# GpSimd forms the difference of the real and the imaginary spectrum once a step, and layer 0's first matmul reads it

## The chip, the cores and the metric

The kernel runs on one core of a Trainium2 chip. The metric is the device time of one execution in microseconds; the number quoted for a kernel is the median of its runs. Besides, one execution is profiled, and all durations below come from that one.

## The reference, cut to what matters

Two spectral layers run one after the other on an image tensor of 4 x 45 x 90 x 384 (batch, height, width, channel). The channels fall into 8 blocks of 48.

```python
# layer 0
f  = fft2(x, axes=(1, 2), norm='ortho')
Xh = f.real - f.imag                      # only 23 of the kw columns are kept
o1 = relu(einsum('bhwni,nio->bhwno', Xk, w1[0]) + b1[0])
o2 = einsum('bhwni,nio->bhwno', o1, w2[0]) + b2[0]
x  = ifft2(softshrink(o2), ...).real + x
# layer 1
xf  = rfft2(x); xr, xi = xf.real, xf.imag
o1r = relu(xr@w1[0] - xi@w1[1] + b1[0]);  o1i = relu(xi@w1[0] + xr@w1[1] + b1[1])
o2r = softshrink(o1r@w2[0] - o1i@w2[1] + b2[0]);  o2i = softshrink(o1i@w2[0] + o1r@w2[1] + b2[1])
out = irfft2(o2r + 1j*o2i) + x
```

Layer 0's first product needs only the difference of the real and the imaginary part. The kernel stays in the spectrum between the layers: layer 1's spectrum is layer 0's input spectrum with the real part of layer 0's result added.

## The kernel before, in words

The work is cut into 8 tasks (4 batches by 2 halves of 192 channels), and each task into 6 steps of 4 columns kw of the spectrum, the last one of 3 (`STEP`, `kws(s)`). There are so 48 steps, 8 of them short. All data are float32. One list, `order`, made by `schedule()` (L103), is walked by every engine, and each engine issues its own part of each entry, so an engine's queue is in the order of the list. The entries are:

- `fwd`: the DFT along the width on TensorE (PE, L566), copied by ScalarE (ACT, L401) into `fs` and stored to a scratch in DRAM by SyncE (SP).
- `load` and `a`: SP loads the rows of a step into `bt`, PE makes the DFT along the height (L612), and ACT (L410) and VectorE (DVE, L482) copy one half each of the channel pairs into `xs[s % 2]`. Its last axis holds 45 real values and then 45 imaginary ones.
- `c0`: layer 0's first product (L630). Four 64 x 64 matmuls, one for each block of a half task, take the real half with the weights `w10[0]`, and four more take the imaginary half with `w10[1]`, which is the negated copy that DVE makes once (L469, tile `w10_neg`, "w_neg" in the rows). They accumulate in two PSUM banks. ACT (L416) and DVE (L486) make the relu into `o10`.
- `d0`: layer 0's second product (L641), four matmuls on `o10`, of the same shape as one half of `c0`. ACT (L421) and DVE (L494 to L504) shrink it into `nt`. Then GpSimd (POOL, L362) subtracts `nt`, which holds the negated result, from the real half of `xs`.
- `c1`, `d1`: layer 1's two products (L653, L666), with relu by ACT (L428) and DVE (L511), and shrinking by ACT (L435) and DVE (L519) into `ns`.
- `t`: transposes of `nt` (L679), added to `ns` by DVE (L527).
- `e`: inverse DFT along the height (L692), copied by ACT (L441) and DVE (L534), stored to a scratch.
- `rows`, `inv`: the inverse DFT along the width (L599), added to the image by DVE (L545). POOL issues the store of each chunk of 8 image rows (L371) and, once an earlier chunk's store has landed, the load of a later task's rows into the same place (`refill`, L352). The first six steps each also issue a load of a third image from POOL (L365).

A profile counts two records for each float32 matmul, so a line of four matmuls shows as x8.

Within step s the list is: load(s+2), c1(s-1), inv, e(s-2), inv, c0(s), d1(s-1), d0(s), fwd, fwd, a(s+1), fwd, fwd, t(s-1), inv; the `fwd` entries are there in three steps of six and the `inv` entries in others. So PE has t, c1, e and perhaps inverse work between `a` of a step and `c0` of the same step:

```python
        if s < NSTEPS:
            order.append(("c0", s))
        if 0 < s <= NSTEPS:
            order.append(("d1", s - 1))
        if s < NSTEPS:
            order.append(("d0", s))
```

The first step is different: the list begins with all of task 0's `fwd`, load(0), load(1), a(0), then c0(0), d0(0), a(1), c1(0), c0(1), d1(0), with nothing between a(0) and c0(0).

## Time and profile before

| | |
|---|---|
| median of 3 runs | 551.11 us (551.05 to 554.34) |
| the profiled execution's own time | 549.69 us |
| its span in the profile | 547.9 us |
| PE busy | 506.0 us, 92% |
| DVE / ACT / POOL busy | 56% / 38% / 25% |
| mean granted clock | 0.97 of full |

The profiled execution's time is 1.8 us above its span, and 1.4 us below the median. A row's line number (L630) is a line of the kernel before. PE is the matmuls, PEld its weight loads, "idle before" the time an engine sat idle just before an instruction, with what released it. Busy time of matmuls that overlap is counted once, while the mean of one is its full length in the pipeline.

### The profile page before, as it was taken

To read this page: it belongs to the slowest core of one execution; us is meant where nothing else is said; L and a number is where in the kernel's file an instruction comes from. 1 tells how busy PE (TensorE), PEld (TensorE's weight loads), DVE (VectorE), ACT (ScalarE), POOL (GpSimd) and SP (SyncE) were. 2 spreads that over 40 slices of the span, in tenths; PEclk is the share of its full clock that TensorE was granted. 3 is DMA by queue.
4 is the path that set the end of the run, shared out by engine and by line. 5 is a ranking of instruction groups with operands and counts; after the bars stand their busy time and mean duration, and the time that the engine had idled before them with its cause. 6 is when DMAs were issued, how large, how long until landed. Compare 5 with 4: busy or idle time off the path is not lost.

```text
span 547.9 us, 14234 instructions
## 1 busy us (share of the span) xinstructions
PE 506.0 (92%) x5824; PEld 372.7 (68%) x5824; DVE 305.5 (56%) x675; ACT 210.9 (38%) x473; POOL 135.6 (25%) x146
## 2 busy tenths in 40 slices
PE   4559999999999999999999999999999999999763
PEld 1147777767777777777777777777777777887521
DVE  6414455456754667456763577456764577556643
ACT  0015544553344433554245433444345434343201
POOL 9701211012330132212331133211331111111124
PEclk9759999999999999999999999999999999999978
DMA  8869764576889578886889588886889655633388
GB/s 184 260 155 245 204 173 109 112 206 173 237 214 239 147 192 246 212 203 173 251 200 228 156 205 237 220 200 168 249 202 220 178 159 150 152 95 101 107 222 252
DMA packets 76717, 104.60 MB, mean 191 GB/s; under 512 B 7761, under 2 KB 63303, under 8 KB 76526
## 3 DMA queue, kind: packets, MB, share of 16 engines
q1 hardware_dynamic: 57622, 55.97, 38.9%
q0 software_dynamic: 10608, 40.45, 28.4%
q10 hardware_dynamic: 8424, 7.28, 5.2%
q8 instruction: 47, 0.77, 0.6%
q14 instruction: 16, 0.13, 0.1%
HBM read 52.23 MB, written 51.43 MB: 189 GB/s over the span
## 4 chain that ended last, share of the span: by engine, by line
PE 84%; DVE 5%; DMA 3%; POOL 3%; ACT 2%; issue 2%; SPq 0%; POOLq 0%; ACTq 0%; DVEq 0%
PE ps L666 15%; PE ps L599 13%; PE ps L566 11%; PE ps L692 11%; PE ps L653 11%; PE ps L612 9%; PE ps L630 7%; PE ps L679 5%; PE ps L641 3%; DVE img L545 2%; DMA scr_f<-fs 2%; DVE ns L519 1%; POOL img L379 1%; ACT p L435 1%; POOL xs L362 1%
## 5 line engine op out<-in xcount | busy, mean ns | idle before, releaser
L545 DVE TENSOR_TENSOR img<-ps,img 90x768 f32<-90x768 f32 x92 | 82.7, 900 | 21.7 <-PE ps L599 17.0
L362 POOL TENSOR_TENSOR xs<-xs,nt 128x360 f32<-128x360 f32 (+1 forms) x48 | 41.5, 864 | 212.1 <-DVE nt L497 134.2
L599 PE MATMUL ps<-jr,cst 64*128 64x384 f32 (+1 forms) x358 | 82.5, 528 | 6.7 <-DVE img L545 5.9
L666 PE MATMUL ps<-wt,o 128*109 128x96 f32 (+1 forms) x768 | 85.4, 263 | 0.1
L666 PEld LDWEIGHTS ps<-wt,o 128*109 128x109 f32 (+1 forms) x768 | 76.4, 171 | 13.3 <-issue 12.5
L519 DVE SCALAR_TENSOR_TENSOR ns<-p,ps 109x384 f32<-109x384 f32 x96 | 53.1, 553 | 57.2 <-ACT p L435 57.2
L566 PE MATMUL ps<-img,cst 128*64 128x384 f32 (+1 forms) x368 | 74.0, 520 | 11.4 <-DMA img<-x 7.6
L612 PEld LDWEIGHTS ps<-cst,bt 128*64 128x64 f32 x1472 | 63.2, 141 | 20.6 <-issue 13.9
L371 POOL DMA_DIRECT2D y<-img x42 | 34.7, 827 | 170.7 <-DVE img L545 170.7
L428 ACT ACTIVATE o<-ps,wt 97x180 f32<-97x180 f32 (+1 forms) x96 | 33.8, 406 | 108.8 <-PE ps L653 108.8
L612 PE MATMUL ps<-cst,bt 128*64 128x90 f32 x1472 | 69.0, 248 | 6.3 <-DMA bt<-scr_f 6.3
L692 PE MATMUL ps<-ns,cst 64*90 64x192 f32 x736 | 70.9, 322 | 0.0
L653 PE MATMUL ps<-xs,wt 64*97 64x180 f32 (+1 forms) x768 | 67.7, 313 | 2.8 <-POOL xs L362 2.5
L692 PEld LDWEIGHTS ps<-ns,cst 64*90 64x90 f32 x736 | 62.6, 155 | 7.7 <-issue 1.5
L653 PEld LDWEIGHTS ps<-xs,wt 64*97 64x97 f32 x768 | 56.7, 159 | 13.3 <-POOL xs L362 6.7
L435 ACT ACTIVATE p<-ps 109x384 f32<-109x384 f32 x96 | 47.1, 491 | 38.4 <-PE ps L666 38.4
L566 PEld LDWEIGHTS ps<-img,cst 128*64 128x64 f32 x368 | 25.5, 144 | 40.7 <-issue 34.8
L511 DVE TENSOR_SCALAR o<-ps,wt 97x180 f32<-97x180 f32 (+1 forms) x96 | 33.7, 393 | 32.6 <-PE ps L653 32.6
L401 ACT ACTIVATE fs<-ps 112x384 f32<-112x384 f32 x84 | 39.1, 476 | 33.3 <-PE ps L566 26.9
L482 DVE COPY xs<-ps 128x360 f32<-128x360 f32 (+1 forms) x48 | 24.8, 516 | 44.0 <-PE ps L612 44.0
L527 DVE TENSOR_TENSOR ns<-ps,ns 109x192 f32<-109x192 f32 x96 | 29.8, 352 | 33.5 <-PE ps L679 32.7
L599 PEld LDWEIGHTS ps<-jr,cst 64*128 64x128 f32 x358 | 31.8, 190 | 24.1 <-issue 12.0
(43 smaller groups left out, 411.9 us busy)
## 6 DMA issues: line engine op xcount, KB each, us to landing
y<-img POOLq DMA_DIRECT2D x35, 540.0 KB, 5.1
img<-x POOLq DMA_DIRECT2D x30, 540.0 KB, 8.3
scr_i<-et SPq DMA_DIRECT2D x48, 270.0 KB, 5.8
scr_f<-fs SPq DMA_DIRECT2D x176, 72.0 KB, 3.0
bt<-scr_f SPq DMA_DIRECT2D x40, 270.0 KB, 4.6
jr<-scr_i SPq DMA_DIRECT2D x48, 216.0 KB, 5.3
img<-x ACTq DMA_DIRECT2D x10, 540.0 KB, 6.7
y<-img SPq DMA_DIRECT2D x11, 270.0 KB, 3.6
```

What stands on the lines that cost most here:

```text
L362: nc.gpsimd.tensor_tensor(re, re, nt[s % 2][:, :, 0:kws(s), 0:H], ALU.subtract).then_inc(re_ok, 1)
L401: nc.scalar.activation(fs[k][0:rows, 0:cols], ps[0:rows, P3 + g % 2, 0:cols], ACT.Copy).then_inc(f_cp, 1)
L435: nc.scalar.activation(p1[0:rows, p, :], ps[0:rows, P2 + p, 0:2 * HC], ACT.Relu).then_inc(d1_p, 1)
L519: nc.vector.scalar_tensor_tensor(out=ns[0:rows, p].rearrange("p n r c -> p (n r c)"), in0=p1[0:rows, p, :], scalar=2 * LAM, in1=ps[0:rows, ...
L545: nc.vector.tensor_tensor(y, p, y, ALU.add).then_inc(i_add, 1)
L566: last = mm(ps[64 * r:64 * r + 64, P3 + g % 2, 0:(b - a) * HC], K["w_fwd"], img[t % IMGS][:, a:b, :].rearrange("p h c -> p (h c)"), start= ...
L599: last = mm(ps[:, B0 + r, 0:n], K["w_inv"][64 * r:64 * r + 64, :], set_rows(t, j)[64 * r:64 * r + 64, at, 0:n], start=True, stop=True)
L612: last = mm(ps[64 * ab:64 * ab + 64, P0 + q, k * 2 * H:(k + 1) * 2 * H], bt[s % BT][:, at:at + 64], K["h_fwd"], start=True, stop=True)
L630: last = mm(ps[64 * q:64 * q + 64, P1 + ab, 0:n], w10[im][k, f, q, :], xt[k, q, 0:kws(s), im * H:(im + 1) * H], start=im == 0, stop=im == 1)
L653: last = mm(ps[0:2 * BS + 1, P2 + ab, q * STEP * H:q * STEP * H + n], w1[k, im, 2 * f + q, :], xt[k, q, 0:kws(s), im * H:(im + 1) * H], st ...
L666: last = mm(ps[0:rows, P2 + p, b * 2 * BS:(b + 1) * 2 * BS], o11[:, b, 2 * p:2 * p + kw, :].rearrange("p k m -> p (k m)")[:, 0:rows], w21[ ...
L692: last = mm(ps[0:2 * H, P0 + r, p * HC:(p + 1) * HC], K[("h_inv_re", "h_inv_im")[im]][k, :], ns[k, p, :, im, :], start=im == 0, stop=im == 1)
```

## The change

Once a step, in the `a` entry, POOL waits for both copies into `xs` and subtracts the imaginary half from the real half into a new tile `xd` (128 x 360 values, 128 x 270 in a short step). `c0` waits for that difference alone and runs four matmuls on it instead of eight on the two halves; the negated weights and the instruction that made them are gone. POOL's older subtraction from `xs` (in `d0`) loses its own two waits on the copies, which now stand ahead of it in POOL's queue. The difference is one buffer: the next one is written after `a` of the next step, which on PE comes behind the `c0` that reads it.

```diff
--- before.py
+++ after.py
@@ -168,7 +168,7 @@
         for n, m in WCOLS.items():
             V[n] = wt[:, at:at + m]
             at += m
-        w10 = [V["w10"].rearrange("p (f q o) -> p f q o", f=HALVES, q=2), sb("w10_neg", [128, HALVES, 2, 64])]
+        w10 = V["w10"].rearrange("p (f q o) -> p f q o", f=HALVES, q=2)
         w20 = V["w20"].rearrange("p (f q o) -> p f q o", f=HALVES, q=2)
         w1 = V["w1"].rearrange("p (r n o) -> p r n o", r=2, n=HALVES * 2)
         w21 = V["w21"].rearrange("p (n o) -> p n o", n=NBLK)
@@ -176,6 +176,7 @@
         fs = [sb(f"fs{k}", [128, 2 * HC]) for k in range(FS)]
         bt = [sb(f"bt{k}", [128, STEP * HC + 16]) for k in range(BT)]
         xs = [sb(f"xs{k}", [128, 2, STEP, 2 * H]) for k in range(2)]
+        xd = sb("xd", [128, 2, STEP * H])
         o10 = sb("o10", [128, 2, STEP * H])
         p0 = sb("p0", [128, 2, STEP * H])
         ev = sb("ev", [128, 2, H])
@@ -204,6 +205,7 @@
         f_st = [sem(f"f{k}_stored") for k in range(FS)]
         b_ld = [sem(f"b{k}_loaded") for k in range(BT)]
         a_mm, a_act, a_dve = sem("a_product"), sem("a_copied_act"), sem("a_copied_dve")
+        xd_ok = sem("re_minus_im")
         c0_mm, c0_act, c0_dve = sem("c0_product"), sem("c0_relu_act"), sem("c0_relu_dve")
         d0_mm, d0_p, d0_ss, d0_ev, d0_sym, re_ok = (sem("d0_product"), sem("d0_clipped"), sem("d0_shrunk"), sem("d0_kw0_shrunk"),
                                                   sem("d0_kw0_even"), sem("re_added"))
@@ -352,10 +354,15 @@
                     pool.dma_start(img[k][0:W, r0:r1, :], x[b, r0:r1, :, f * HC:(f + 1) * HC].rearrange("h w c -> w h c")).then_inc(x_ld[k][c], 16)
 
             for kind, *what in order:
-                if kind == "d0":
+                if kind == "a":
                     s, = what
                     pool.wait_ge(a_act, s + 1)
                     pool.wait_ge(a_dve, s + 1)
+                    xt = xs[s % 2][:, :, 0:kws(s), :]
+                    nc.gpsimd.tensor_tensor(xd[:, :, 0:kws(s) * H].rearrange("p q (k m) -> p q k m", m=H), xt[:, :, :, 0:H], xt[:, :, :, H:2 * H],
+                                            ALU.subtract).then_inc(xd_ok, 1)
+                if kind == "d0":
+                    s, = what
                     pool.wait_ge(d0_ss, 2 * s + 2)
                     pool.wait_ge(d0_sym, 2 * (s // STEPS + 1))
                     re = xs[s % 2][:, :, 0:kws(s), 0:H]
@@ -466,7 +473,6 @@
                 if kind == "load" and what[0] == 0:
                     dve.wait_ge(c_ld, 16)
                     dve.wait_ge(w_ld, 16)
-                    nc.vector.tensor_scalar(w10[1][:], w10[0], -1.0, None, ALU.mult).then_inc(w_ok, 1)
                     v = w20[:, :, :, 0:BS].rearrange("p f n o -> p (f n) o")
                     nc.vector.tensor_scalar(v, v, K["lam"], 0.5, ALU.add, ALU.mult).then_inc(w_ok, 1)
                     v = w1[0:112, 1, :, 0:BS]
@@ -475,7 +481,7 @@
                     nc.vector.tensor_scalar(v, v, K["sign"][0:2 * BS, :], None, ALU.mult).then_inc(w_ok, 1)
                     v = w21[2 * BS:2 * BS + 1, :, :]
                     nc.vector.tensor_scalar(v, v, LAM, None, ALU.add).then_inc(w_ok, 1)
-                    dve.wait_ge(w_ok, 5)
+                    dve.wait_ge(w_ok, 4)
                 if kind == "a":
                     s, = what
                     dve.wait_ge(a_mm, 2 * s + 2)
@@ -614,21 +620,18 @@
                         last.then_inc(a_mm, 1)
                 if kind == "c0":
                     s, = what
-                    n, f, xt = kws(s) * H, s // STEPS % HALVES, xs[s % 2]
+                    n, f = kws(s) * H, s // STEPS % HALVES
                     if s == 0:
-                        pe.wait_ge(w_ok, 5)
-                    pe.wait_ge(a_act, s + 1)
-                    pe.wait_ge(a_dve, s + 1)
+                        pe.wait_ge(w_ok, 4)
+                    pe.wait_ge(xd_ok, s + 1)
                     if s > 0:
                         pe.wait_ge(d0_ss, 2 * s)
                     if s > 1:
                         pe.wait_ge(t_add, 2 * s - 2)
-                    for im in range(2):
-                        for ab in range(2):
-                            for q in range(2):
-                                k = slice(64 * ab, 64 * ab + 64)
-                                last = mm(ps[64 * q:64 * q + 64, P1 + ab, 0:n], w10[im][k, f, q, :], xt[k, q, 0:kws(s), im * H:(im + 1) * H],
-                                          start=im == 0, stop=im == 1)
+                    for ab in range(2):
+                        for q in range(2):
+                            k = slice(64 * ab, 64 * ab + 64)
+                            last = mm(ps[64 * q:64 * q + 64, P1 + ab, 0:n], w10[k, f, q, :], xd[k, q, 0:n], start=True, stop=True)
                     last.then_inc(c0_mm, 1)
                 if kind == "d0":
                     s, = what
```

PE's queue in one middle step, in issue order: t (L679), c1 (L653), inverse groups (L599), e (L692), c0 (L630), d1 (L666), d0 (L641). Before:

```order
L679 MATMUL ps<-cst,nt 109x128 x4
L653 MATMUL ps<-xs,wt 97x180 x8
L599 MATMUL ps<-jr,cst 128x384 x2
L692 MATMUL ps<-ns,cst 90x192 x8
L599 MATMUL ps<-jr,cst 128x384 x2
L630 MATMUL ps<-xs,wt 64x180 x4
L630 MATMUL ps<-xs,w_neg 64x180 x4
L666 MATMUL ps<-wt,o 109x96 x8
L641 MATMUL ps<-o,wt 64x180 x4
```

The same place on PE now; c0 is L634, d1 L669, d0 L644:

```order
L682 MATMUL ps<-cst,nt 109x128 x4
L656 MATMUL ps<-xs,wt 97x180 x8
L605 MATMUL ps<-jr,cst 128x384 x2
L695 MATMUL ps<-ns,cst 90x192 x8
L605 MATMUL ps<-jr,cst 128x384 x2
L634 MATMUL ps<-xd,wt 64x180 x4
L669 MATMUL ps<-wt,o 109x96 x8
L644 MATMUL ps<-o,wt 64x180 x4
```

The four matmuls with the negated weights are gone, and nothing else moved on PE.

POOL's queue over the start of the inverse work of a task, before: the subtraction of `nt` (L362), stores of image chunks (L371) and refills (L352):

```order
L362 TENSOR_TENSOR xs<-xs,nt 128x8x45
L371 DMA y<-img 90x8x192
L352 DMA img<-x 90x8x192
L362 TENSOR_TENSOR xs<-xs,nt 128x8x45
L371 DMA y<-img 90x8x192
L352 DMA img<-x 90x8x192
L371 DMA y<-img 90x8x192
L352 DMA img<-x 90x8x192
L362 TENSOR_TENSOR xs<-xs,nt 128x2x3x45
L371 DMA y<-img 90x8x192
```

The same place on POOL now; L362 is the new difference into `xd`, L369 the subtraction of `nt`, L378 the store, L354 the refill:

```order
L369 TENSOR_TENSOR xs<-xs,nt 128x8x45
L362 TENSOR_TENSOR xd<-xs 128x360
L378 DMA y<-img 90x8x192
L354 DMA img<-x 90x8x192
L369 TENSOR_TENSOR xs<-xs,nt 128x8x45
L362 TENSOR_TENSOR xd<-xs 128x2x135
L378 DMA y<-img 90x8x192
L354 DMA img<-x 90x8x192
L378 DMA y<-img 90x8x192
L354 DMA img<-x 90x8x192
L369 TENSOR_TENSOR xs<-xs,nt 128x2x3x45
L362 TENSOR_TENSOR xd<-xs 128x360
```

One difference for the next step stands directly behind each subtraction of `nt`, ahead of the stores and refills that follow.

POOL's first instructions of the main loop, now (L372 is the load of the third image, L365 before):

```order
L362 TENSOR_TENSOR xd<-xs 128x360
L369 TENSOR_TENSOR xs<-xs,nt 128x8x45
L372 DMA img<-x 90x8x192
L362 TENSOR_TENSOR xd<-xs 128x360
L369 TENSOR_TENSOR xs<-xs,nt 128x8x45
L372 DMA img<-x 90x8x192
```

The first difference has nothing ahead of it but the clears, and the second stands behind the issue of a load.

## Rows read from the trace of the kernel before

**Rows 1.** The page: busy time of each engine, and the chain by engine and line
```profile
PE 506.0 (92%) x5824; PEld 372.7 (68%) x5824; DVE 305.5 (56%) x675; ACT 210.9 (38%) x473; POOL 135.6 (25%) x146
...
PE 84%; DVE 5%; DMA 3%; POOL 3%; ACT 2%; issue 2%; SPq 0%; POOLq 0%; ACTq 0%; DVEq 0%
PE ps L666 15%; PE ps L599 13%; PE ps L566 11%; PE ps L692 11%; PE ps L653 11%; PE ps L612 9%; PE ps L630 7%; PE ps L679 5%; PE ps L641 3%; DVE img L545 2%; DMA scr_f<-fs 2%; DVE ns L519 1%; POOL img L379 1%; ACT p L435 1%; POOL xs L362 1%
```

**Rows 2.** Windows, 100 us each: busy us of PE, PEld, DVE, ACT, POOL, clock, DMA share, GB/s
```profile
200.00:300.00 100.00, 99.17 (x1190) 74.26 (x1190) 58.58 (x134) 43.31 (x98) 25.84 (x31) 1.00 0.84 213
...
400.00:500.00 100.00, 98.16 (x1220) 76.01 (x1217) 59.24 (x140) 42.89 (x97) 17.52 (x22) 1.00 0.63 161
```

**Rows 3.** Chain that ended last, 279 to 294 us: start us, us on the chain, what
```profile
283.24 0.78 PE ps L630 x16
284.01 1.90 PE ps L666 x16
285.92 0.47 PE ps L641 x8
```

**Rows 4.** Same chain, 252 to 270 us, a step of three columns kw
```profile
265.16 0.62 PE ps L630 x16
...
267.48 0.39 PE ps L641 x8
```

**Rows 5.** Groups by line and shape: busy us, mean ns, idle before and its releaser
```profile
L362 POOL TENSOR_TENSOR xs<-xs,nt 128x360 f32<-128x360 f32 x40 | 35.7, 892 | 197.8 <-DVE nt L497 132.3 <-DVE nt L504 45.5 <-ACT xs L410 19.9
...
L630 PE MATMUL ps<-xs,w_neg 64*64 64x180 f32 x320 | 19.9, 317 | 0.0
```

**Rows 6.** Timeline, 83 to 90 us: start us, us, engine, line, operation, idle before
```profile
84.35 0.49 DVE L497 SCALAR_TENSOR_TENSOR nt<-p,ps 128x135 f32<-128x135 f32 x2
...
85.09 0.73 POOL L362 TENSOR_TENSOR xs<-xs,nt 128x270 f32<-128x270 f32 x1 [6.16 <-ACT xs L410]
85.15 0.53 DVE L482 COPY xs<-ps 128x360 f32<-128x360 f32 x1 [0.30 <-PE ps L612]
...
85.77 0.82 POOL L365 DMA_DIRECT2D img<-x  x1
...
85.87 1.17 PE L653 MATMUL ps<-xs,wt 64*97 64x135 f32 x16
...
87.09 0.62 DVE L511 TENSOR_SCALAR o<-ps,wt 97x135 f32<-97x135 f32 x2 [0.71 <-PE ps L653]
...
88.28 0.54 PE L630 MATMUL ps<-xs,wt 64*64 64x180 f32 x8
```

**Rows 7.** Chain in the first steps, columns as in rows 3
```profile
35.11 1.51 PE ps L630 x16
...
37.19 0.88 PE ps L641 x8
```

**Rows 8.** Timeline of the first steps, columns as in rows 6
```profile
34.43 0.53 DVE L482 COPY xs<-ps 128x360 f32<-128x360 f32 x1 [7.16 <-PE ps L612]
...
39.76 0.89 POOL L362 TENSOR_TENSOR xs<-xs,nt 128x360 f32<-128x360 f32 x1 [16.08 <-DVE nt L504]
40.59 0.96 POOL L365 DMA_DIRECT2D img<-x  x1
...
42.23 0.54 PE L630 MATMUL ps<-xs,wt 64*64 64x180 f32 x8
42.36 0.72 ACT L428 ACTIVATE o<-ps,wt 97x180 f32<-97x180 f32 x2 [2.37 <-PE ps L653]
```

**Rows 9.** Windows of 2 us in the first steps, columns as in rows 2
```profile
38.00:40.00 2.00, 2.00 (x30) 2.00 (x28) 0.96 (x6) 0.94 (x2) 0.24 (x1) 0.50 0.29 56
...
42.00:44.00 2.00, 1.86 (x28) 1.32 (x25) 1.12 (x3) 1.13 (x3) 0.00 (x0) 1.00 0.91 232
```

**Rows 10.** Waits: engine, line, for whom: us in total, times, longest us
```profile
POOL img L352 <- DMA y<-img: 18.3, 7, 4.1
...
PEld ps L653 <- POOL xs L362: 6.7, 16, 0.8
```

## Prediction, made before the changed kernel ran

> **What bounds the kernel now.** I read the page's busy times and its chain of waits first [rows 1]: PE is busy 92% of the span and holds 84% of the chain that ended last; no other engine has more than 5% of it. L630, the line that the change cuts, has 7% of the chain. An average over stages can mislead, so the windows come next [rows 2]: between 200 and 300 us PE is busy for 99.2 us and between 400 and 500 us for 98.2, both at the full granted clock (1.00, the 2.4 GHz level). The middle of the program is all like that, so PE's own order of work is the bound, and what counts is how much sooner PE's next instruction starts. Busy time can't give that, since these matmuls overlap: one of L630 takes some 0.31 us from end to end [rows 5], while sixteen of them hold the chain for 0.78 us [rows 3]. The chain in order of time is the view that gives the pitch, and I take the sum from it.
>
> **Part 1, removed: half of c0's matmuls.** In a full step c0 holds the chain for 0.78 us (283.24, x16 records), then d1's L666 follows [rows 3]. What will eight records of this shape take? d0 is just that: four matmuls, 64 x 64 weights, 180 columns, no accumulation. It holds the chain for 0.47 us (285.92, x8) [rows 3]. Half of 0.78 would be 0.39, but a row of the right count and shape stands in the same trace, so I take 0.47: a saving of 0.31 us a step. The next line after d0 is another than after c0; I take the same handover. In a short step the two are 0.62 and 0.39 us [rows 4], a saving of 0.23. Of the 48 steps the first two are priced by themselves below; 38 full and 8 short ones are left: 38 x 0.31 + 8 x 0.23 = 11.8 + 1.8 = 13.6 us. A reader who took the busy time of the removed group would say 19.9 us for the 40 full steps alone [rows 5], some 23 us with the short ones; that counts the pipeline's fill and drain, which lie beside the neighbours' work, and I keep it only as the far end of what is possible. The near end is 0: that these matmuls already ran in the shadow of the others.
>
> **Part 2, added: POOL's difference.** It has the same 128 x 360 values and two inputs as the subtraction at L362, 892 ns each [rows 5], so I take 0.89 us, some 42 us of POOL time in all, against POOL's 25% busy now. It costs time only if c0 has to wait for it. The step with the least room behind the first two is the one at 85 us [rows 6]. POOL ends its subtraction of `nt` at 85.09 + 0.73 = 85.82, and its next item is the issue of a load (85.77, 0.82), which ends at 86.59; DVE's copy into `xs` has ended at 85.68. The difference then runs to 86.59 + 0.89 = 87.48, and c0 starts at 88.28: 0.8 us are left. Only the first six steps issue such a load. I went through all steps behind them the same way, and the room is 1.8 us at the least and 5.0 at the most. The cover is PE's own t, c1 and e, which stand between `a` and c0; if it were gone, each step would pay up to 0.89 us plus the start of an instruction, 0.25 us (DVE's last part of `nt` ends at 84.35 + 0.49 = 84.84, POOL starts at 85.09 [rows 6]), and the gain would turn into a loss.
>
> **What is queued behind the new wait on POOL.** Behind it stand the store of a finished image chunk, the refill, and the next subtraction of `nt`, for which c1 waits (PEld, 6.7 us in 16 waits [rows 10]). The new wait is for copies that are made before that step's t and c0, and every store behind it needs an inverse product that PE makes later than `a`. So the wait is over before a store is due, and a store goes out at most one difference (0.89 us) late; the images have most of a task's time to land. The refills wait for landed stores (18.3 us in 7 waits, the longest 4.1 [rows 10]), but in the queue they stand ahead of the subtraction of `nt` already today, and the difference comes right behind that one: what would delay it delays c1 first, and PE hardly waits there. I cost it at 0, with half a microsecond as the other end.
>
> **Part 3, the first two steps.** Nothing stands between a(0) and c0(0), so there the difference is bare. DVE's copy ends at 34.43 + 0.53 = 34.96 [rows 8] and c0 starts at 35.11 [rows 7]. Now: 34.96, plus 0.25 until POOL starts, plus 0.89, plus 0.05 until PE starts (85.82 to 85.87 [rows 6]) is 36.15, so +1.04. At the half clock of this stretch (0.50 from 38 to 40 us, the 1.2 GHz level [rows 9]) the cut is worth more: c0 holds the chain for 1.51 us and the eight records of d0 for 0.88 [rows 7], so -0.63. Step 0 nets +0.41. In step 1, POOL's subtraction (39.76, 0.89) and the issue of a load behind it (40.59, 0.96) [rows 8] both move by 0.41, so that the load is issued at 41.96; the difference ends at 42.85, and c0 starts at 42.90 where without the wait it would start at 42.64: +0.26. Its own cut of 0.31 is of no use in full, since d1 must wait for layer 1's relu anyway (42.36 + 0.72 = 43.08 [rows 8], now 0.41 later). I take +0.4 us for both steps together. The clock could make it dearer: it stands at 0.50 until 40 us and at 1.00 from 42 on, behind a stretch in which PE was nearly always busy [rows 9]. The microsecond of idle PE at 35 us may move the rise. Were 4 us more spent at the half clock, that would cost 2 us. That is my upper end for it, and I take 0.
>
> **Part 4, small things.** The one DVE instruction for the negated weights lies in a stretch where PE waits for the first load; it is worth 0. PE's wait for one semaphore in place of two is worth 0 as well, because no idle time of PE at L630 shows in the chain. DVE's and ACT's relus of c0 need to be ready for d0, which stands behind d1's 1.90 us [rows 3]; c0 shorter by 0.31 does not touch that. d1 itself needs layer 1's relus: DVE ends them at 87.09 + 0.62 = 87.71 [rows 6], and d1 starts behind c0 at 88.28 + 0.78 = 89.06. Being 0.31 us sooner leaves a microsecond. So nothing is late next.
>
> **The sum.** -13.6 + 0.4 = -13.2 us. Against the profiled execution's own 549.69 us that is 536.5. The median of the runs shown, 551.11, is 1.4 us above that execution; taken from it the result is 537.9 us, my forecast, 2.4% less. No change can be told from a difference under about 1%, 5.5 us.
>
> **Rivals.** (a) *DVE is blocked while POOL reads SBUF.* This is the one on the other side. If each difference held up a DVE instruction on which PE waits, for its whole 0.89 us, 48 of them would cost 42.7 us, and the time would be 537.9 + 42.7 = 580.6. It decides from 13.2 / 48 = 0.28 us a step on. The place would be t's additions (L527) or an inverse addition (L545), which come just behind `a`. For it: POOL's share grows from 25% to some 33%, and the steps put the difference there. Against it: DVE's copy at 85.15 ran its whole length beside POOL's subtraction (85.09 to 85.82) and took 0.53 us [rows 6]; at 34.43, with POOL idle, it took 0.53 us too [rows 8]. The Trainium skill ("SBUF — State Buffer", "SBUF: two separate sides") says that a GpSimd op and a DVE op with two SBUF inputs, or in a two-port mode, exclude each other for their whole length. By that rule the DVE operations here that read PSUM are free, with which the row agrees; only the two small additions of `ev` in every sixth step have two SBUF inputs, and they stand ahead of POOL's work.
>
> (b) *Other waits appear once PE is quicker*, so that half of the gain is given back: 551.1 - 6.6 = 544.5. For it: PE waits now and then for POOL's subtraction [rows 10]; the chain holds 5% of DVE and 3% of POOL [rows 1], and DMA is busy up to 84% in the middle [rows 2]. Against: those waits hang on d0, d1 and inverse products, which all move together with c0, and PE is idle for no more than 1.8% of the middle stretches [rows 2].
>
> (c) *The removed matmuls cost nothing*, since a new matmul is let in by something else than the count: 551.1 + 0.4 = 551.5. For it: four blocks lie in different quarters of the array and overlap. Against: d0's 0.47 against c0's 0.78 on the same chain [rows 3].
>
> (d) *The gain is larger*, toward the busy time: 551.1 - 23 + 0.4 = 528.5. Against: the same two rows.
>
> **Chances.** Forecast 0.82; (b) 0.09; (c) 0.04; (a) 0.03; (d) 0.02. The range runs from 534.5 (a saving of 0.36 a step, no price at the start, and the scatter of a median) to 543.0 (the late clock, the delayed stores, and most of (b)). Faster by over 1% (under 545.6): 0.92, the forecast, (d) and most of (b). Within 1%: 0.05. Slower: 0.03.
>
> **What would show it.** Right: L634 holds the chain for 0.47 us with x8 records where L630 held it for 0.78; c0 never waits for POOL but in the first two steps; POOL's new line is 0.89 us each; DVE's L482, L527 and L545 keep their lengths; PE stays above 98% busy in the middle at clock 1.00. Wrong: PE idle before L634 with POOL as the releaser in most steps (then the room was misread), longer DVE operations (rival a), PE idle at t or c1 that was not there before (b), or a chain in which L634 still holds 0.7 us (c).

## The result

| | before | changed |
|---|---|---|
| median | 552.54 us (551.05 to 554.34, 4 runs) | 536.11 us (535.78 to 537.09, 4 runs) |
| the profiled execution's own time | 549.69 us | 537.09 us |
| its span | 547.9 us | 535.3 us |

The ratio is 0.9704 with a 95% interval of 0.9664 to 0.9745: the change makes the kernel 3.0% faster. The forecast was 537.9 us with a range of 534.5 to 543.0, so the time lies in the range, 1.8 us under the forecast. The two profiled executions differ by 12.6 us and the medians by 16.4: the profiled run of before is 2.9 us under its median, that of the changed kernel 1.0 over its own. The experiments say part of why. Ratios and spreads here are of fast runs alone; three slow runs of the kernel before (558.05, 559.73 and 1225.76 us, all in later sessions) are left out.

The page of the changed kernel, busy times and the chain by engine and line:

```profile
PE 492.0 (92%) x5440; PEld 359.2 (67%) x5440; DVE 304.1 (57%) x674; ACT 209.5 (39%) x473; POOL 172.9 (32%) x194
...
PE 83%; DVE 5%; DMA 5%; POOL 2%; issue 2%; ACT 2%; SPq 0%; POOLq 0%; DVEq 0%; ACTq 0%
PE ps L669 15%; PE ps L605 13%; PE ps L572 12%; PE ps L695 12%; PE ps L656 11%; PE ps L618 9%; PE ps L682 5%; PE ps L634 4%; PE ps L644 3%; DMA scr_f<-fs 2%; DVE img L551 2%; DVE ns L525 2%; POOL xs L369 1%; ACT p L442 1%; DVE nt L503 1%
```

PE is 92% busy as before [rows 1], over a span shorter by 12.6 us; POOL went from 25% to 32%. The changed line, L634 now, has 4% of the chain where L630 had 7%.

The windows of 100 us, columns as in [rows 2]:

```profile
200.00:300.00 100.00, 99.22 (x1140) 73.75 (x1141) 59.69 (x138) 44.40 (x101) 32.06 (x39) 1.00 0.84 219
...
400.00:500.00 100.00, 97.14 (x1144) 73.98 (x1143) 61.83 (x140) 42.37 (x98) 24.59 (x30) 1.00 0.58 153
```

PE is the bound as before, at the full granted clock. The prediction wanted it above 98% in both windows; in the second it is 97.14, because the 1.28 us for which PE waits behind the last d0 (at 494.3 us now, 507.7 before) have moved into that window. The chain in the middle, to be held against [rows 3]:

```profile
277.33 0.47 PE ps L634 x8
277.79 1.70 PE ps L669 x16
279.49 0.47 PE ps L644 x8
```

L634 holds the chain for 0.47 us with x8 records (0.78 with x16 before), and d0 behind it (L644) for 0.47 as it did. The short step, against [rows 4]:

```profile
259.81 0.39 PE ps L634 x8
```

The timeline of the step with the least room, against [rows 6]:

```profile
84.13 0.49 DVE L503 SCALAR_TENSOR_TENSOR nt<-p,ps 128x135 f32<-128x135 f32 x2
...
84.70 0.73 POOL L369 TENSOR_TENSOR xs<-xs,nt 128x270 f32<-128x270 f32 x1 [5.08 <-DVE nt L503]
...
84.93 0.53 DVE L488 COPY xs<-ps 128x360 f32<-128x360 f32 x1 [0.30 <-PE ps L618]
85.37 0.82 POOL L372 DMA_DIRECT2D img<-x  x1
...
85.49 1.17 PE L656 MATMUL ps<-xs,wt 64*97 64x135 f32 x16
...
86.21 0.83 POOL L362 TENSOR_TENSOR xd<-xs 128x360 f32<-128x360 f32 x1
...
87.89 0.54 PE L634 MATMUL ps<-xd,wt 64*64 64x180 f32 x8
```

The difference (L362 now) is done at 87.04 and L634 starts at 87.89: 0.85 us of room, where 0.8 was forecast. One thing was not forecast: POOL's subtraction (L369) starts at 84.70, 0.08 us behind its last input (84.13 + 0.49 = 84.62). Before, it was 0.25 us [rows 6].

I took the start of d0's first weight load in each of the 48 steps of both profiles and compared step by step (steps counted from 0). Most full steps are 0.31 to 0.34 us shorter and the short ones 0.23. Steps 44 to 46, and 6, are 0.45 to 0.48 shorter, and the short steps 5 and 47 by 0.39 and 0.38. Steps 18 and 25 are 0.44 and 0.53 shorter. Step 15 gains 0.16, and steps 12 and 31 only 0.05; in these two PE has a wait at c1 (L656) that it did not have before. One of them, step 12:

```profile
143.02 0.81 POOL L354 DMA_DIRECT2D img<-x  x1 [2.12 <-DMA y<-img]
...
143.84 0.74 POOL L369 TENSOR_TENSOR xs<-xs,nt 128x270 f32<-128x270 f32 x1
...
144.64 1.17 PE L656 MATMUL ps<-xs,wt 64*97 64x135 f32 x16 [0.51 <-POOL xs L369]
```

POOL's refill waited 2.12 us for a store to land, and so its subtraction, for which c1 waits, came late. In the second profile of the changed kernel this step is 0.32 shorter, like the others. The other one is step 31: PE waits 0.28 us at 334.85, since the subtraction starts 0.44 us behind its last input where it starts 0.15 behind it in the like steps; it starts as DVE's copy ends. That is so in experiments 1, 2, 10 and 11 too, and why is open.

By stretches, in us, with the second profile of the changed kernel (the first experiment):

| stretch | before | changed | changed, again |
|---|---|---|---|
| to a(0) | 31.64 | 31.28 | 31.35 |
| a(0) to d0(1) | 13.25 | 14.71 | 13.49 |
| d0(1) to d0(2) | 10.26 | 9.94 | 9.94 |
| d0(2) to d0(46), 44 steps | 442.72 | 428.91 | 428.59 |
| d0(46) to d0(47) | 9.33 | 8.95 | 8.94 |
| d0(47) to the end | 40.70 | 41.51 | 41.16 |
| span | 547.9 | 535.3 | 533.5 |

### The profile page after: what moved, and what is told of

Its sections match the earlier page's. It is cut to its first block, busy times and chain, and to the rows that moved or that the text cites. A ratio compares the mean times of both kernels' runs of the same rounds, so it can differ in the third digit from the quotient of the medians.

```text
span 535.3 us, 13467 instructions
## 1 busy us (share of the span) xinstructions
PE 492.0 (92%) x5440; PEld 359.2 (67%) x5440; DVE 304.1 (57%) x674; ACT 209.5 (39%) x473; POOL 172.9 (32%) x194
## 4 chain that ended last, share of the span: by engine, by line
PE 83%; DVE 5%; DMA 5%; POOL 2%; issue 2%; ACT 2%; SPq 0%; POOLq 0%; DVEq 0%; ACTq 0%
PE ps L669 15%; PE ps L605 13%; PE ps L572 12%; PE ps L695 12%; PE ps L656 11%; PE ps L618 9%; PE ps L682 5%; PE ps L634 4%; PE ps L644 3%; DMA scr_f<-fs 2%; DVE img L551 2%; DVE ns L525 2%; POOL xs L369 1%; ACT p L442 1%; DVE nt L503 1%
## 5 line engine op out<-in xcount | busy, mean ns | idle before, releaser
L369 POOL TENSOR_TENSOR xs<-xs,nt 128x360 f32<-128x360 f32 (+1 forms) x48 | 41.6, 866 | 160.0 <-DVE nt L503 130.6
L605 PE MATMUL ps<-jr,cst 64*128 64x384 f32 (+1 forms) x358 | 84.2, 540 | 6.9 <-DVE img L551 5.6
L669 PE MATMUL ps<-wt,o 128*109 128x96 f32 (+1 forms) x768 | 85.2, 263 | 0.5 <-DVE o L517 0.5
L669 PEld LDWEIGHTS ps<-wt,o 128*109 128x109 f32 (+1 forms) x768 | 76.3, 171 | 13.3 <-issue 12.6
L572 PE MATMUL ps<-img,cst 128*64 128x384 f32 (+1 forms) x368 | 72.2, 507 | 13.3 <-DMA img<-x 7.7
L378 POOL DMA_DIRECT2D y<-img x42 | 34.6, 825 | 132.4 <-DVE img L551 132.1
L656 PE MATMUL ps<-xs,wt 64*97 64x180 f32 (+1 forms) x768 | 68.9, 317 | 2.4 <-POOL xs L369 2.3
L656 PEld LDWEIGHTS ps<-xs,wt 64*97 64x97 f32 x768 | 57.5, 161 | 13.3 <-POOL xs L369 6.7
L362 POOL TENSOR_TENSOR xd<-xs 128x360 f32<-128x360 f32 (+1 forms) x48 | 38.0, 792 | 34.4 <-DVE xs L488 34.3
```

Source lines behind the costliest of these rows:

```text
L362: nc.gpsimd.tensor_tensor(xd[:, :, 0:kws(s) * H].rearrange("p q (k m) -> p q k m", m=H), xt[:, :, :, 0:H], xt[:, :, :, H:2 * H], ALU.subtr ...
L369: nc.gpsimd.tensor_tensor(re, re, nt[s % 2][:, :, 0:kws(s), 0:H], ALU.subtract).then_inc(re_ok, 1)
L572: last = mm(ps[64 * r:64 * r + 64, P3 + g % 2, 0:(b - a) * HC], K["w_fwd"], img[t % IMGS][:, a:b, :].rearrange("p h c -> p (h c)"), start= ...
L605: last = mm(ps[:, B0 + r, 0:n], K["w_inv"][64 * r:64 * r + 64, :], set_rows(t, j)[64 * r:64 * r + 64, at, 0:n], start=True, stop=True)
L656: last = mm(ps[0:2 * BS + 1, P2 + ab, q * STEP * H:q * STEP * H + n], w1[k, im, 2 * f + q, :], xt[k, q, 0:kws(s), im * H:(im + 1) * H], st ...
L669: last = mm(ps[0:rows, P2 + p, b * 2 * BS:(b + 1) * 2 * BS], o11[:, b, 2 * p:2 * p + kw, :].rearrange("p k m -> p (k m)")[:, 0:rows], w21[ ...
```

## The experiments

**1. The changed kernel again.** No edit.

> The changed kernel itself, timed in one session with the next three and with the kernel before. By the traces the step saves 0.31 us 38 times and 0.23 us 8 times and the first two steps lose 1.5 us, so 12 to 13.5 us less than before (ratio 0.975 to 0.978). If the medians' 16.4 us are real and not scatter of the kernel before, the ratio is 0.970 again.

Measured: 536.28 us, ratio 0.9709 (0.9672 to 0.9746). The second alternative came true: the ratio is 0.970 again. But the stretch with the 44 steps is 428.59 us, 14.1 less than in the profile of before, while the ratio makes 16 us. The rest lies outside these profiles, in runs of before that are slower than its profiled one (see experiment 5).

**2. The difference formed, and read by nobody.** The kernel before, with

```diff
+                if kind == "a":
+                    s, = what
+                    pool.wait_ge(a_act, s + 1)
+                    pool.wait_ge(a_dve, s + 1)
+                    if s > 0:
+                        pool.wait_ge(xd_ok, s)
+                    nc.gpsimd.tensor_tensor(xd ..., re, im, ALU.subtract).then_inc(xd_ok, 1)
                 if kind == "d0":
                     s, = what
-                    pool.wait_ge(a_act, s + 1)
-                    pool.wait_ge(a_dve, s + 1)
```

> The kernel before, with GpSimd forming the difference of each step at the same place in its queue, but nobody reads it: the first product still runs eight matmuls on the two halves. Theory (the difference is hidden and slows no other engine): within 1 us of the kernel before, DVE's copy at 0.53 us, its additions at 0.62 us a pair and 0.95 us as before. Rival (DVE is blocked while GpSimd reads SBUF): DVE operations beside the difference grow by up to 0.83 us, and the time by over 5 us.

Measured: 550.4 us, ratio 0.9961 (0.993 to 0.9992). The groups by line and shape of this kernel:

```profile
L555 DVE TENSOR_TENSOR img<-ps,img 90x768 f32<-90x768 f32 x84 | 79.8, 953 | 21.0 <-PE ps L609 16.3
...
L364 POOL TENSOR_TENSOR xd<-xs 128x360 f32<-128x360 f32 x40 | 32.8, 820 | 35.8 <-ACT xs L420 22.6 <-DVE xs L492 10.7 <-issue 2.4
...
L537 DVE TENSOR_TENSOR ns<-ps,ns 109x192 f32<-109x192 f32 x88 | 27.7, 353 | 33.4 <-PE ps L689 32.7
...
L492 DVE COPY xs<-ps 128x360 f32<-128x360 f32 x40 | 21.3, 532 | 44.4 <-PE ps L622 44.4
```

The difference takes 0.82 us, and DVE's copy (532 ns), its additions behind the transposes (353) and behind the inverse (953) are what they were. The rival is out for operations that read PSUM. The stretch of 44 steps is 442.43 us against 442.72, so the difference is close to free: two steps are longer, 31 by 0.26 us as in the changed kernel, and 38 by 0.58. Steps 5, 6 and 44 to 47 are 0.14 to 0.16 us shorter: the same surplus that the changed kernel shows there. The ratio says some 2 us less than before (0.4%, between 0.1 and 0.7), more than the 1 us that the theory allowed; the surplus of six steps is 0.9 us of it.

**3. Half the product alone.** The kernel before, with `for im in range(1)` in c0 and `start=True, stop=True`. It leaves out the imaginary half of layer 0's input.

> The kernel before with only the real half of the first product: four matmuls in place of eight, no difference, no new wait; it leaves out the imaginary part of layer 0's input. It prices the cut alone. Theory: 0.47 us on the chain in a full step, 0.39 in a short one, 0.6 us saved in the first step, so 14 us under the kernel before and 1 to 2 us under the changed kernel, all of that in the first two steps. Rival (GpSimd's difference costs something in the middle too): the steps from the third on are shorter than the changed kernel's by more than 0.03 us each.

Measured: 537.23 us, ratio 0.9732 (0.9693 to 0.977). Without any difference on POOL, the last steps (40 to 47) are 0.31 and 0.22 or 0.23 us shorter than before, each of them, with no surplus. So the cut is worth what the row of d0 said. The rival is out: of the steps from the third on only 12, 15 and 31 are shorter than the changed kernel's by more than 0.03 us (0.26, 0.15 and 0.26), and against its second profile only 15 and 31. Steps 18 and 25 are 0.44 and 0.51 us shorter here too, so their extra belongs to the profile of before and not to POOL. The kernel is 1.0 us slower than the changed one, not 1 to 2 us faster as the theory had it; the runs of the two overlap. Three things that the rows show go into that. The surplus of 0.15 us is missing. The stretch behind the last d0 is 43.03 us here against 41.51 and 41.16: the granted clock is 0.88 from 494 to 498 us and 0.69 from 498 to 502, where both profiles of the changed kernel have 1.00. And the start is no better. In its chain the first steps read

```profile
35.72 0.91 PE ps L630 x8
...
37.20 0.88 PE ps L641 x8
...
40.70 2.65 PE ps L653 x16
```

L653's sixteen records in step 1 last 2.65 us here, though no bare wait for POOL stands ahead of them.

**4. The first two steps as of old.** The changed kernel, with c0 of steps 0 and 1 on the two halves, waiting for the copies, and the difference from step 2 on:

```diff
-                    pe.wait_ge(xd_ok, s + 1)
+                    if s < 2:
+                        pe.wait_ge(a_act, s + 1)
+                        pe.wait_ge(a_dve, s + 1)
+                    else:
+                        pe.wait_ge(xd_ok, s - 1)
```

> The changed kernel, but the first two steps use the two halves and the negated weights as before, and the difference begins with the third step. Theory (the loss at the start comes from the bare wait for GpSimd and from the clock that rises later behind it): L653's sixteen records in step 1 last 1.6 us as before and not 2.7, and the kernel is 1.0 to 1.5 us under the changed one. Rival (the clock's rise in that stretch varies from run to run whatever the code): no difference that holds, or L653's line still at 2.7 us.

Measured: 535.18 us, ratio 0.969 (0.9649 to 0.9731), 1.1 us under the changed kernel timed beside it; the two intervals overlap for the most part, so I call it a hint. L671, layer 1's product in step 1, lasts 2.47 us: the clock rises late here too, without the bare wait. In the second profile of the changed kernel, with the bare wait, it rises early (a(0) to d0(1) in 13.49 us, table above). In the second profile of the kernel before, which has no bare wait either, it rises late (14.16 us for that stretch, 13.25 in the first; experiment 5). The rival holds: the clock's rise moves by some 2 us between profiles of one and the same kernel.

**5. The kernel before again.** No edit.

> The kernel before, profiled a second time, for where its runs scatter (549 to 557 us in the last session). Theory: the middle (from the third d0 to the 47th) is 442.7 us again within 0.3, and the scatter lies in the first 45 us and behind the last d0. Rival: the middle differs by over 1 us between two profiles, and then a saving read from one profile is not safe.

Measured: 551.76 us, ratio 0.9993. The stretch of 44 steps is 444.06 us, 1.34 more than in the first profile. The rival holds (and the start differs too, as just said), and the profile shows the place. In its chain:

```profile
221.75 0.78 PE ps L630 x14
222.53 1.18 issue
223.71 0.47 PE ps L630 x2
224.17 1.70 PE ps L666 x16
```

PE stops for 1.18 us inside c0 of step 19 (counted from 0; the expectations of experiments 9 and 10 call it 18), behind the 14th of its 16 records, and the profile shows nothing that it waits for ("issue"). Step 19 as a whole is 1.63 us longer than in the first profile. The other 43 steps are the same within 0.2 us.

**6. The waits moved alone.** The kernel before, where POOL's two waits for the copies stand in the `a` entry, with nothing else there.

> The kernel before with one thing of the change alone: GpSimd's two waits for the copies stand in the a entry, ahead of the stores, and not in front of its subtraction; no difference is formed. In the profiles so far GpSimd starts that subtraction 0.24 us (median) behind its last input where four waits stand in front of it, and 0.09 us behind it where two do. Theory (the shorter start helps where layer 1's product waits for GpSimd, some 15 to 20 steps): lag 0.09, and 1 to 2.5 us under the kernel before, like the kernel with the unread difference. Rival (that kernel's 0.4% is scatter, or the difference itself does it): no change, under 0.5 us.

Measured: 550.99 us, ratio 0.9991 (0.9967 to 1.0014). POOL's subtraction starts 0.09 us (median) behind its last input, where it was 0.24. But only steps 44 and 47 are shorter, by 0.16 and 0.14 us, where experiment 2 had six such steps. The lags say why. Where nothing stands in POOL's queue between the `a` entry and the subtraction, all four waits stand in a row again, and the lag is 0.23 or 0.24 as of old: so ahead of steps 5, 6, 45 and 46, and not ahead of 44 and 47. This settles that the surplus comes from the waits and not from the difference. The theory got the mechanism right and its worth wrong: only in these few steps does POOL's start set d0's time, and elsewhere 0.15 us there buys nothing. This profile has the gap of experiment 5 at the same instruction, and larger, and it costs more than its length:

```profile
220.59 0.77 PE ps L632 x14
221.36 2.02 issue
223.37 0.47 PE ps L632 x2
223.84 2.66 PE ps L668 x16
226.50 0.81 PE ps L643 x8
```

```profile
222.00:224.00 2.00, 0.63 (x4) 0.36 (x4) 0.12 (x1) 0.12 (x1) 0.00 (x0) 1.00 0.64 132
224.00:226.00 2.00, 2.00 (x15) 2.00 (x15) 0.69 (x2) 0.78 (x2) 0.81 (x1) 0.59 0.86 264
226.00:228.00 2.00, 2.00 (x15) 0.99 (x16) 0.82 (x3) 0.96 (x2) 0.00 (x0) 0.55 0.74 211
228.00:230.00 2.00, 2.00 (x40) 1.45 (x38) 0.48 (x2) 1.31 (x3) 0.89 (x1) 1.00 0.06 17
```

Behind 2.02 us of idle PE the mean granted clock of the next two windows is 0.59 and 0.55, so it stood at the half level (0.50, 1.2 GHz) for some 3.4 of these four microseconds, and d1 takes 2.66 us in place of 1.70. Step 19's d0 comes 3.4 us late in all.

**7. Four differences in a row.** The changed kernel; from step 8 on three more differences go into a tile of their own first:

```diff
+                    for r in range(3 if s >= 8 else 0):
+                        nc.gpsimd.tensor_tensor(xe ..., ALU.subtract).then_inc(xe_ok, 1)
+                        pool.wait_ge(xe_ok, 3 * (s - 8) + r + 1)
```

> The changed kernel, but from the ninth step on GpSimd forms the difference four times in a row, the last one being the one that is read: 2.7 to 2.8 us later. This measures the room that the prediction read from the trace. Theory: the room is about 2 us in each second step of a task (1.8 read from the kernel before, 0.2 more by the shorter start and operation), and also in the last few steps, and 3 us or more in the others; so PE waits 0.7 to 0.8 us for GpSimd in some 8 steps, 6 us in all. Rival (the room is smaller than read): waits in over 20 steps and over 15 us.

Measured: 546.13 us, ratio 0.9901 (0.9873 to 0.9929); 9.9 us over the changed kernel. From its waits:

```profile
PE ps L639 <- POOL xd L367: 10.3, 15, 1.8
```

PE waits 15 times for the difference, the 1.8 us at the start among them. Step by step against the changed kernel, seven of the theory's eight places (13, 19, 25, 37 and 43 to 45) come 0.75 to 0.79 us late, as worked out from a room of 2.0, and the eighth (31) 0.47. But six more (12, 14, 20, 26, 32, 38) are 0.5 to 1.0 us late, where I had read 3 us of room or more. The theory's 6 us became 9.9, still far from the rival's 15. POOL's timeline at the largest one:

```profile
218.59 0.82 POOL L383 DMA_DIRECT2D y<-img  x1
...
224.40 0.80 POOL L355 DMA_DIRECT2D img<-x  x1 [4.15 <-DMA y<-img]
225.22 0.90 POOL L374 TENSOR_TENSOR xs<-xs,nt 128x360 f32<-128x360 f32 x1
226.07 2.63 POOL L364 TENSOR_TENSOR xe<-xs 128x360 f32<-128x360 f32 x3
228.77 0.82 POOL L367 TENSOR_TENSOR xd<-xs 128x360 f32<-128x360 f32 x1
```

In the changed kernel the store of that stretch is issued at 215.05; here it is issued at 218.59, of which the three extra differences ahead of it make 2.6 us. The refill behind it needs a landed store and so comes at 224.40 (220.38 there), the subtraction of `nt` right behind it, and only then four more differences. The room read from a profile holds for a delay that leaves the rest of the queue where it is; one that moves the queue's stores eats more than itself.

**8. The difference on DVE.** The changed kernel, with the same `tensor_tensor` behind DVE's copy in place of POOL's. POOL's subtraction of `nt` then waits for the difference besides, so it has three waits in front of it.

> The changed kernel with the difference on VectorE, right behind its copy, in place of GpSimd. Theory: an operation of some 0.45 us, which no trace here shows yet; in steps without forward work the additions behind the transposes follow DVE's copy within 0.1 us and have 0.35 us of room before e, so they come late by 0.1 to 0.2 us in some 20 steps; the start is better by 0.4 us; 0 to 3 us slower than the changed kernel. Rival (a faster engine is the better place): up to 1 us faster.

Measured: 537.59 us, ratio 0.9745 (0.9717 to 0.9773), 1.3 us slower than the changed kernel by the medians (of two sessions). The timeline of two steps:

```profile
152.94 0.88 POOL L363 TENSOR_TENSOR xs<-xs,nt 128x360 f32<-128x360 f32 x1 [3.48 <-DVE nt L509]
...
153.31 0.90 DVE L486 TENSOR_TENSOR xd<-xs 128x360 f32<-128x360 f32 x1
...
154.14 0.61 DVE L532 TENSOR_TENSOR ns<-ps,ns 109x192 f32<-109x192 f32 x2
```

```profile
162.66 0.53 DVE L486 TENSOR_TENSOR xd<-xs 128x360 f32<-128x360 f32 x1
```

Alone the difference takes 0.53 us, shorter than POOL's 0.82. But at 153.31 it takes 0.90: POOL's subtraction runs until 153.82, and DVE's ends 0.39 us behind that. Of its 48 instances the sixteen that begin well inside such a subtraction last 0.81 to 1.06 us; four that begin in its last 0.18 us last 0.53 to 0.58, like the others. All twenty end 0.29 to 0.42 us behind the end of POOL's subtraction. So a DVE operation with two inputs in SBUF is kept out while a GpSimd one runs. The Trainium skill ("SBUF — State Buffer", "SBUF: two separate sides") says that whichever of the two starts first keeps the other out; the trace agrees for GpSimd first, and no run here has the other order. This is rival (a) of the prediction, alive in the place where its rule has it. The additions behind the transposes then start late, and in these steps d0 comes 0.05 to 0.2 us later, twice by more (0.36 and 0.67). POOL's subtraction starts 0.15 us (median) behind its last input, and steps 44 to 46 are 0.41 or 0.42 us shorter than before, so they keep 0.10 of the surplus of 0.15. The Trainium skill's "GPSIMD Engine Reference" ("Engine selection") puts elementwise work on VectorE, as GpSimd is about twice as slow with two inputs. Here it is 1.5 times as slow (0.82 against 0.53 us), and DVE's speed is of no use, for the time is set elsewhere.

**9. The old stream shifted.** The kernel before, with 32 matmuls of two columns in PE's wait for the first load:

```diff
+                    if s == 0:
+                        for r in range(32):
+                            mm(ps[0:2, P2 + r % 2, 0:2], cst[0:64, 0:2], cst[0:64, 0:2], start=True, stop=True)
```

> The kernel before with 32 tiny matmuls (128 instructions, two columns each) put into TensorE's wait for the first load, so that all later TensorE instructions stand 128 places further in its stream. Two of four profiles with the old TensorE stream show TensorE idle for 1.2 and 2.0 us at the same instruction, behind the 14th record of c0 in step 18, with nothing waited for. Theory (the next block of instructions comes late there, where the DMA engines are at their busiest): with the stream shifted no such gap at that place, runs from 549 to 552 and a median 1 to 2 us under the kernel before. Rival (the gap belongs to that moment or to the work, not to the place in the stream): the gap is at the same instruction again, or the spread of 549 to 558 us stays.

Measured: 551.79 us, ratio 0.9991 (0.9968 to 1.0013), runs from 550.1 to 554.4. The profile has no gap at that place, and its 44 steps take 443.05 us. The runs of before beside it go from 549.3 to 554.8 with a median of 552.3, 0.5 us above this kernel's, well inside the interval and less than the 1 to 2 us of the theory. a(0) starts at 33.33 here and not at 31.64, which may hide up to 1.7 us of gain. The fillers' own length is not what delays it: they were done at 27.1, and a(0) waited for the first load of `bt`, which landed later. So it is in all four kernels with fillers (32.45 to 33.57, against 30.91 to 32.25 in the ten profiles without), and why is open. Step 12 is 0.65 us longer here than in the first profile, since PE waits 0.89 us for POOL behind a refill that waited for a landed store, as in the changed kernel. The theory is neither borne out nor refuted.

**10. The new stream set back.** The changed kernel with 76 such matmuls at the same place.

> The changed kernel with 76 tiny matmuls (304 instructions) in TensorE's wait for the first load, about as many as the change removes before step 18, so that the stream around step 18 has its old alignment again. Theory (late instruction block): the gap of 1 to 2 us can come back in c0 or d1 of step 18, runs spread over 3 us or more and the median is 1 us or more above the changed kernel's 536.2 (up to 1 us of it may be the filler itself, read from the start of a(0)). Rival: no gap, spread 2 us as before.

Measured: 536.79 us, ratio 0.972 (0.9695 to 0.9746), four runs within 1.3 us; no gap. The theory's guess that the alignment alone brings the gap back fell, as far as one profile and four runs can tell. It may be that a gap needs dense transfers at that moment as well, and here c0 of step 19 comes 4.5 us earlier (216.5 against 221.0); no run shows this.

**11. Fillers for the clock.** The changed kernel with 36 matmuls of 180 columns in PE's wait for the first load and 8 ahead of the first difference.

> The changed kernel with matmuls that nobody reads in two idle stretches of TensorE at the start: 36 of 180 columns in its wait for the first load (25 to 31 us), and 8 in the bare wait for the first difference. Theory (the clock is at half speed from 31 to 41 or 43 us because TensorE was idle before): the granted clock is 1.00 from a(0) on, a(0) takes 1.3 us and not 2.7, L656's line in step 1 takes 1.6, and the time is 3 to 4 us less. Rival (the clock rises late whatever is done there, as it varied between profiles of one kernel): clock 0.50 at 32 to 40 us again and no gain; if the fillers themselves run at half speed they end near 33 us and cost up to 2 us.

Measured: 536.29 us, ratio 0.9707 (0.9681 to 0.9734): no gain. The windows of 2 us:

```profile
26.00:28.00 2.00, 2.00 (x60) 2.00 (x56) 1.27 (x4) 0.00 (x0) 0.00 (x0) 1.00 0.55 151
28.00:30.00 2.00, 0.44 (x12) 0.11 (x4) 0.00 (x0) 0.00 (x0) 0.00 (x0) 1.00 0.03 4
30.00:32.00 2.00, 0.00 (x0) 0.00 (x0) 0.00 (x0) 0.00 (x0) 0.00 (x0) 0.69 0.62 177
...
34.00:36.00 2.00, 2.00 (x29) 1.69 (x29) 0.47 (x1) 0.47 (x1) 0.00 (x0) 0.50 0.20 25
36.00:38.00 2.00, 1.57 (x20) 0.55 (x12) 0.13 (x2) 0.00 (x1) 0.82 (x1) 0.60 0.98 268
38.00:40.00 2.00, 1.51 (x34) 1.28 (x36) 0.76 (x4) 1.04 (x3) 0.00 (x0) 1.00 0.54 121
```

The fillers ran at the full clock and were done at 28.4; PE was then idle until 32.74, and the clock was at half again when a(0) came (2.69 us). It did rise earlier behind that, before 38 us, where the profiles of the changed kernel have 0.50 from 38 to 40. But a(0) had started 1.5 us later than in the changed kernel (see experiment 9). The gain that the theory names was not had, and the theory itself was not put to the test, for the filler was too short for the wait.

**12. Fillers and the old start.** Experiment 4 with the 36 fillers.

> The changed kernel with the two halves of old in the first two steps, which was 1.1 us faster, and the 36 filler matmuls in TensorE's wait for the first load. Theory: both gains add, 4 to 5 us under the changed kernel, 531 to 532 us. Rival: with the clock up, the bare wait for GpSimd is all that is left of the first one, so it is 0.5 us better than the kernel with both fillers, no more.

Measured: 536.55 us, ratio 0.9714 (0.9689 to 0.9739). No gain either: a(0) starts at 33.57 us, 2.4 later than in experiment 4, and at half clock.

## Why the prediction was right, and where it was off

**The bound** was PE's own order of work, as read from [rows 1, 2]: what the cut frees on PE's chain came out of the time almost whole. The ratio's 3.0% is more than the 2.4% forecast, and that the time is still only 1.8 us off owes something to luck in the base: the forecast stood on a median of 551.11, and with a fourth run it is 552.54.

**Part 1** (0.31 us a full step, 0.23 a short one, from the row of d0) was exact. Experiment 3 shows it by itself, in steps 40 to 47: 0.31 and 0.22 to 0.23. The busy time of the removed group, some 23 us, would have been wrong by 9 us. It was right to take the pitch from the chain.

**Part 2** (the difference hidden, room of 0.8 us at the least) held: the room measured is 0.85, PE waits for POOL at L634 once in the whole run, 1.8 us in step 0; in the second profile there is one more wait, 0.27 us in step 1, where 0.26 was worked out. The difference takes 0.82 us and not 0.89. Experiment 2 shows that it costs next to nothing by itself (0.26 us in step 31 is the one price that comes back), experiment 7 that the room in the second step of a task is as read, and that the larger room of other steps is not to be had in full.

**Part 3**: step 0 lost 0.40 us against a forecast of 0.41 (d0(0) at 37.21 after a(0) at 31.28, against 37.17 after 31.64). Step 1 lost 1.06 in the first profile, where about nothing was forecast for it alone, and gained 0.15 in the second. That is the clock, for which up to 2 us stood in the range. The reason given, the microsecond of idle PE, is not borne out, though: experiments 3 and 4 and the second profile of the kernel before have no bare wait and the same late rise.

**Part 4** was off by its one sentence that a wait fewer is worth 0. It looked at PE's waits and not at POOL's. POOL's subtraction of `nt` had four waits in front of it and now has two, the others being over before; it starts 0.15 us sooner, and in steps 5, 6 and 44 to 47, where c1 stands waiting for it, that comes off the time. 37 full and 7 short steps at the forecast's rate make 13.1 us; the profiles show 13.8 and 14.1. Of the surplus 0.3 us is steps 18 and 25, where the first profile of before is long by itself (its second is 0.12 and 0.20 us shorter there); five of the six steps with the shorter start lie in the stretch and give 0.8; step 31, and 12 and 15 in the first profile, take some back. Experiment 2 shows the 0.15 us with PE's work unchanged, and experiment 6 that the waits alone make it.

**The sum and the reference.** -13.2 was forecast between two profiles, and -12.6 and -14.4 were measured (spans 535.3 and 533.5 against 547.9). What the sum did not hold is that runs of before scatter upward, from 549.3 to 557.0 us over the sessions, with medians of 551.8 to 552.5, while the changed kernel stays within 535.3 and 537.2. The median of three runs, 551.11, was low for it. One cause of the scatter is seen: two of the four profiles whose PE stream is that of before (the two of the kernel itself, experiments 2 and 6) have a gap at one and the same instruction, of 1.2 and of 2.0 us, the second with a fall of the clock behind it; none of the other profiles has one of more than 0.25 us in the middle. What makes the gap is argued and not shown: a block of instructions that comes late. Each kernel's instruction queue moves blocks of 0.02 MB, one of them between 220 and 222 us in both profiles with the gap. The traces say more: that block starts to move at 220.88 and 220.74 us in the profiles with the gap, 1.7 and 0.6 us ahead of the stop, and PE goes on 2.8 and 2.6 us behind its start; in the two profiles of that stream without the gap (the first one and experiment 2) it starts at 218.55 and 217.68, over 3 us ahead of the same instruction. That fits a late block and does not prove it, nor does it say why the block is late. The Trainium skill ("Runtime: NRT & Kernel Launch", "Instruction fetch mechanics") has blocks of 16 KiB that are fetched while the engine runs and are mostly hidden. Experiments 9 and 10 did not settle it. PE's waits behind a late refill (0.89 us in experiment 9, 1.02 in experiment 11) are another part of the scatter, in both kernels. How much of the 2 to 4 us between the medians' and the profiles' difference either carries stays open.

**The rivals.** (a) did not occur, for the reason given, and experiment 8 shows that its mechanism is real. (b) hardly occurred: PE's new waits in the middle are the 0.51 and 0.28 us at c1, 0.8 us in all and 0.28 in the second profile. (c) and (d) are out by the chain.

## What to carry to other kernels

When PE is the bound, price a removed matmul by how long such a group holds the chain, from a row with the same count and shape, and not by its busy time. An idle engine can take over linear work ahead of a matmul if the queue position leaves room; look at the tightest step, at the steps with extra work in that queue, and at the start, where nothing covers it, and mind which other operations the engine's new one collides with: the faster engine can be the worse place. Compare medians over enough runs of both kernels: the one with the wider scatter moves the ratio by more than a few tenths of a per cent.

## What the runs showed of the hardware

- With four waits in front of it GpSimd's subtraction started 0.24 us (median) behind its last input, with three 0.15 (experiment 8), with two 0.09.
- A DVE operation with two SBUF inputs was kept out while GpSimd ran, and took 0.90 us in place of 0.53; operations that read PSUM were not (a copy 0.53 us beside it and alone, additions 353 and 953 ns with and without the difference).
- GpSimd's subtraction from one tile into a new one took 0.82 us, the one that reads two tiles and writes over one of them 0.89, at the same 128 x 360 values; which of these makes the difference no run shows.
- PE stopped in the middle of a group with nothing to wait for (1.18 and 2.02 us), and the stop of 2.02 us was followed by some 3.4 us at the half clock, the one of 1.18 by none.
- The clock's rise at the start moved by some 2 us between two profiles of one kernel: from 40 to 42 us the mean granted clock was 0.75 and 0.50 in those of the kernel before, 0.50 and 0.86 in those of the changed one.
